# Two-phase kernel on Trainium2: output projection of a batch placed in the next batch's first tail, and end turns without absent groups

## The reference, cut to what matters

```python
q, k, v = (silu(conv4(x @ W)) for W in (Wq, Wk, Wv))   # causal, depthwise
q, k = rope(q), rope(k); q, k = q / norm(q), k / norm(k)
beta, alpha = sigmoid(x @ bw + bb), exp(-exp(A_log) * softplus(x @ gkw + ...))
# per step t:
o_t = q_t S + D * (q_t . k_t) * v_t
S   = alpha_t * (S - beta_t * k_t (k_t S)) + beta_t * k_t v_t
on  = o * rsqrt(mean(o * o) + eps) * onorm_w
s = (g * silu(on)) @ Wo              # g = x @ Wg
```

## Time and profile before

| what | value |
|---|---|
| median of 3 runs | 4598.03 us (4592.21 to 4605.60) |
| the profiled execution | 4639.09 us |
| its span | 4637.3 us, 93208 instructions |
| PE busy | 4129.0 us, 89% |
| PE weight loads | 2724.7 us, 59% |
| DVE / ACT / POOL busy | 65% / 42% / 35% |
| mean granted clock | 0.932 |

### The profile page before, as it was taken

The page is one execution under the profiler, slowest core; times in us unless marked ns, Lnnn a source line. Parts: engine busy times, 40 slices in busy tenths (PEclk is TensorE's granted clock), DMA queues, the critical chain, the costliest instruction groups (busy, mean ns, idle before and its releaser), DMA issues.

```text
span 4637.3 us, 93208 instructions
## 1 busy us (share of the span) xinstructions
PE 4129.0 (89%) x32914; PEld 2724.7 (59%) x32914; DVE 3014.4 (65%) x6409; ACT 1969.6 (42%) x4156; POOL 1644.7 (35%) x1479
## 2 busy tenths in 40 slices
PE   5999998999998989669899899998999989989998
PEld 4444444444444444337667666766666667667666
DVE  3555555555555555377767777867767678678676
ACT  2343334343434343244444534535435445354444
POOL 2111111111111111045545454646554556455454
PEclk9999999999999999888988898988998989989999
DMA  2000000000000000111111111111111111111111
GB/s 97 1 15 1 15 1 15 1 15 1 15 1 15 1 15 1 54 24 39 19 41 26 28 32 23 34 29 30 31 36 19 44 23 30 33 30 23 44 19 34
DMA packets 316505, 110.49 MB, mean 24 GB/s; under 512 B 290096, under 2 KB 303664, under 8 KB 315184
## 3 DMA queue, kind: packets, MB, share of 16 engines
q1 hardware_dynamic: 315968, 103.69, 9.5%
HBM read 77.45 MB, written 26.74 MB: 22 GB/s over the span
## 4 chain that ended last, share of the span: by engine, by line
PE 36%; DVE 11%; issue 4%; ACT 4%; POOL 1%; DMA 1%; SPq 1%; DVEq 0%; POOLq 0%; ACTq 0%
PE d_ps L1778 6%; DVE d_acc L1463 4%; PE d_ps L1854 3%; PE d_ps L1977 3%; PE d_ps L1962 3%; PE d_ps L1997 3%; PE d_ps L1816 2%; PE d_ps L1756 2%; PE d_ps L1833 2%; PE d_ps L1825 1%; PE d_ps L1891 1%; PE d_ps L1905 1%; PE d_ps L1869 1%; DVE d_pw L1566 1%; PE d_ps L1795 1%
## 5 line engine op out<-in xcount | busy, mean ns | idle before, releaser
L228 POOL TENSOR_TENSOR f_qk<-f_m 128x512 f32<-128x512 f32 x128 | 162.8, 1272 | 1538.8 <-DVE f_m L411 1538.7
L1463 DVE SCALAR_TENSOR_TENSOR d_acc<-d_ps,d_cw,d_acc 128x511 f32<-128x511 f32 (+2 forms) x630 | 468.3, 744 | 80.8 <-ACT d_acc L1246 65.0
L1778 PE MATMUL d_ps<-d_xnT,d_wqkv 128*128 128x512 f32 x840 | 488.5, 713 | 0.2 <-DVE d_acc L1463 0.2
L311 ACT ACTIVATE f_pr<-f_sm,f_nb,f_qsc 128x256 f32<-128x256 f32 (+1 forms) x512 | 289.0, 565 | 239.7 <-DVE f_nb L439 237.8
L687 PE MATMUL f_ps<-f_m,f_w 128*128 128x512 f32 (+1 forms) x768 | 338.5, 595 | 22.6 <-DVE f_m L483 22.6
L1246 ACT ACTIVATE d_acc<-d_ps,d_cw 128x512 f32<-128x512 f32 x210 | 162.4, 774 | 406.5 <-PE d_ps L1778 404.6
L1124 POOL TENSOR_TENSOR d_rn<-d_ss,d_mhalf 128x8 f32<-128x8 f32 x137 | 236.5, 1726 | 255.4 <-DVE d_ss L1484 252.3
L433 DVE CUSTOM_DVE_ANT_0 f_sm<-f_ps,f_mask 128x256 f32<-128x256 f32 (+1 forms) x512 | 179.4, 388 | 207.9 <-PE f_ps L603 197.6
L1119 POOL TENSOR_TENSOR d_qk<-d_m 128x512 f32<-128x512 f32 x138 | 174.8, 1267 | 393.4 <-DVE d_m L1474 386.3
L1281 ACT ACTIVATE d_m<-d_qk 128x512 f32<-128x512 f32 x138 | 86.7, 628 | 421.2 <-POOL d_qk L1119 421.2
L687 PEld LDWEIGHTS f_ps<-f_m,f_w 128*128 128x128 f32 (+1 forms) x768 | 134.3, 178 | 223.0 <-issue 187.2
(11 more groups left out here) (210 smaller groups left out, 9675.0 us busy)
## 6 DMA issues: line engine op xcount, KB each, us to landing
d_wqkv<-in_dwqkv SPq DMA_DIRECT2D x36, 768.0 KB, 4.5
blocks_scratch<-d_LT SPq DMA_DIRECT2D x136, 64.0 KB, 2.0
d_T<-inverse_scratch SPq DMA_DIRECT2D x136, 64.0 KB, 2.2
f_xin<-in_x SPq DMA_DIRECT2D x9, 512.0 KB, 4.2
d_xnT<-xnT_scratch SPq DMA_DIRECT2D x9, 512.0 KB, 5.2
d_xnG<-xnT_scratch SPq DMA_DIRECT2D x9, 512.0 KB, 6.6
d_LB<-blocks_scratch SPq DMA_DIRECT2D x68, 64.0 KB, 2.8
inverse_scratch<-d_TB SPq DMA_DIRECT2D x68, 64.0 KB, 4.9
```

The costliest lines, as they stand in the source:

```text
L311: nc.scalar.activation(pr[:, u % 2, j, k0:], sm[:, u % 2, j, k0:], ACT.Exp, bias=nb[:, u % 2, j:j + 1], scale=qsc[:, 0, w, h:h + 1], accum ...
L1463: V.scalar_tensor_tensor(out=a[:, k:], in0=ps[:, CV_BANK[n], 0:T - k], scalar=cw[:, X, s * CT + t, TAPS - 1 - k:TAPS - k], in1=a[:, k:], o ...
L1778: last = mm(ps[:, CV_BANK[n], :], wqkv[:, X, k, t * P:(t + 1) * P], xnT[:, k, :], start=k == 0, stop=k == KC - 1)
```

## The change

It has two parts. The sequence of work is rewritten as a function turn(b, step) on each engine, in which a group that would be outside 0 to 31 is None and its parts are left out. The turns are: step -3 to 0 written out, then a loop over 7 batches with steps 1 to 4 (so the loop's jump comes after the turn s=0 of the next batch), then steps 1 to 3 written out for the last batch. And the output of batch b is placed in the tail of the turn s=0 of batch b + 1; only that of the last batch stays at the end. PE runs the first half of the projection (bank 0) behind convolution item 0, the second half (bank 1) behind item 1, and the transposes, now into banks 0 and 1, behind item 3. To free oT and on, the squares go to a buffer m12 (m1 and m2 side by side), and z is kept in gate. On SP, the store and the next loads of gate and rows stand ahead of inverse_back.

```diff
-    m1 = sb("m1", [P, 2 * GW])
-    m2 = sb("m2", [P, 2 * GW])
+    m12 = sb("m12", [P, 4 * GW])
+    m1, m2 = m12[:, 0:2 * GW], m12[:, 2 * GW:4 * GW]
-    sq = m1
+    sq, osq = m1, m12
-    z = on[:, :, :].rearrange("p (m a) n -> p m (a n)", m=KC)
+    z = gate
+    def group(b, k):
+        if isinstance(b, int) and not 0 <= b * NG + k < B * NG:
+            return None
+        return b * NG + k, k % NG, b + k // NG
+    def late(i, k):
+        return not isinstance(i, int) or i >= k
+    def done(now):
+        return now[2] - 1 if now and now[1] == 0 and late(now[2], 1) else None
     # SP
+        def turn(b, step):
+            now, mid, sub, conv, load = (group(b, step + k) for k in range(5))
+            if sub:
+                inverse_io(sub[0], sub[1] % 2)
+            if conv and load:
+                conv_weights(load[0], load[1])
+            if now and now[1] == 0 and conv:
+                sp.dma_start(flat(xnT), scratch["xnT"][now[2] + 1, :, :, :]).then_inc(xn_in, 16)
...
+            if done(now) is not None:
+                store(done(now))
+                sp.wait_ge(zT_ps, 1 + 2 * now[2])
+                sp.dma_start(flat(gate), scratch["gate"][now[2], :, :, :]).then_inc(gate_in, 16)
+                sp.wait_ge(out_st, 1 + now[2] * 16)
+                sp.dma_start(flat(xio), io["x"][now[2], :, :, :]).then_inc(x_in, 16)
+            if sub:
+                inverse_back(sub[0])
     # ACT, out_heads_T
+            if s == 0 and late(bt, 1):
+                act.wait_ge(wo_ps, 1 + KC * bt)
     # DVE, tail
             if mid: merge16(mid[0])
             conv_items(i, s, range(0, 1))
+            if done(now) is not None: output(done(now), 0)
             conv_items(i, s, range(1, 2))
+            if done(now) is not None: output(done(now), 1)
             merge16_mid, substitute, conv item 2, merge16_end, conv item 3, merge32
+            if done(now) is not None: output_end(done(now))
             substitute_end, merge32_end, ...
     # PE
-                pe.wait_ge(xo_rdy, 1 + 2 * bt)
-        def output(b, i):
-            pe.wait_ge(rf_c, 1 + 2 * (i + 1) + 2)
-            pe.wait_ge(oT_rdy, 1 + b * NG * CT + NG * CT)
-            pe.wait_ge(cv_acc, 1 + val(i + 3, 6, 6))
-            pe.wait_ge(rot_rdy, 1 + 2 * val(i + 3, NT, 2))
+        def output(b, i, m):
+            if m == 0:
+                pe.wait_ge(os_rdy, 1 + val(i, 2 * NT, 2 * NT))
+                pe.wait_ge(oT_rdy, 1 + b * NG * CT + NG * CT)
+            for k in range(H * DH // P):
+                last = mm(ps[:, m, :], wo[:, k, m * P:(m + 1) * P], oT[:, k, :], start=k == 0, stop=k == H * DH // P - 1)
+            last.then_inc(wo_ps, 1)
     # PE, merge32_end
+            if put is not None:
+                pe.wait_ge(xo_rdy, 1 + put * 2 + 2)
     # PE, tail
             conv(*conv_g, 0)
+            if put is not None: output(put, now[0], 0)
             merge16(mid[0], mid[1] % 2, 0)
             conv(*conv_g, 1)
+            if put is not None: output(put, now[0], 1)
             merge16 (second half), g_proj, merge16_end, conv 2, merge16_end, conv 3
+            if put is not None: output_T(put)
             merge32, g_proj, out_heads, merge32_end(mid[0], gated, put), ...
     # every engine
+        for step in range(-3, 1):
+            turn(0, step)
+        with pe.Fori(0, B - 1) as b:
+            for step in range(1, NG + 1):
+                turn(b, step)
+        for step in range(1, NG):
+            turn(B - 1, step)
+        for m in range(KC):
+            output(B - 1, B * NG - 1, m)
+        output_T(B - 1)
```

More of the change, by code:

```diff
@@ new lines, in tail, with turn @@
+            if conv:
+                first_tap(i, s, 4)
+                squares(i, s, bt, 0)
+            if mid:
+                merge64(mid[0])
+            if conv:
+                silu(i, 4)
+                first_tap(i, s, 5)
+            if mid:
+                merge64_end(mid[0])
+            if conv:
+                silu(i, 5)
+                decay_exp(i, s, bt, 0)
+                squares(i, s, bt, 1)
+        def turn(b, step):
+            now, mid, made, conv = (group(b, step + k) for k in range(4))
+            tiles(made, now)
+            tail(conv, mid, now)
@@ L1417, in _ @@
+        act.wait_ge(init1, 1 + 5)
+        for step in range(-3, 1):
+            turn(0, step)
+        with act.Fori(0, B - 1) as b:
+            for step in range(1, NG + 1):
+                turn(b, step)
+        for step in range(1, NG):
+            turn(B - 1, step)
     @block.vector
@@ new lines, in tail @@
+            if conv:
+                i, s, bt = conv
+                conv_items(i, s, range(0, 1))
+            if done(now) is not None:
+                output(done(now), 0)
+            if gated is not None:
+                gates(gated)
+            if conv:
+                conv_items(i, s, range(1, 2))
+            if done(now) is not None:
+                output(done(now), 1)
+            if mid:
+                merge16_mid(mid[0])
+            if sub:
+                substitute(sub[0])
@@ new lines, in tail, with turn @@
+            if conv:
+                intake(i, s, bt, 0)
+                conv_items(i, s, range(4, 5))
+                norms(i, s, bt, 0)
+                intake(i, s, bt, 1)
+                conv_items(i, s, range(5, 6))
+        def turn(b, step):
+            now, mid, made, conv = (group(b, step + k) for k in range(4))
+            tiles(made, now)
+            tail(conv, made, mid, now)
+        dve.wait_ge(init1, 1 + 5)
+        for step in range(-3, 1):
+            turn(0, step)
+        with dve.Fori(0, B - 1) as b:
+            for step in range(1, NG + 1):
+                turn(b, step)
@@ L1726, in _ @@
+        for step in range(1, NG):
+            turn(B - 1, step)
+        for m in range(KC):
+            output(B - 1, m)
+        output_end(B - 1)
     @block.tensor
@@ new lines, in tail, with turn @@
+            if mid:
+                merge64(mid[0], mid[1] % 2)
+            if conv_g:
+                conv(*conv_g, 5)
+                decay_sums(*conv_g, 0)
+            if mid:
+                merge64_end(mid[0])
+        def turn(b, step):
+            now, mid, made, conv_g = (group(b, step + k) for k in range(4))
+            tiles(made, now)
+            tail(conv_g, mid, now)
+        pe.wait_ge(init1, 1 + 5)
+        for step in range(-3, 1):
+            turn(0, step)
+        with pe.Fori(0, B - 1) as b:
+            for step in range(1, NG + 1):
+                turn(b, step)
```

437 lines of the change are left out of this document (189 added, 248 removed).

## The result

The changed kernel takes 4566.85 us (median of 10 runs, 4541.34 to 4594.85) where the kernel before takes 4606.44 beside it (10 runs): a ratio of 0.991 with an interval from 0.988 to 0.994. It is faster, by 40 us where the forecast was 110, and it lies above the range, which ended at 4545.

The account below looks back on a forecast made before the run. The output projection was taken to hold everything up 21.4 us at each batch's end, with PE nearly full in the s=0 tail. Boundary 31, clock 10 and last batch 69 made 110 off 4598: 4488 us, range 4450 to 4545.

Parts of the forecast that it names:

- The sum A to C: Boundary between batches: stall removed, less projection in the s=0 tail and loop's edge, 4.5 a batch, times 7 = 31 us.
- Part A: End of a batch: the stall behind the output projection goes, seven times, mean gain 20.4 us.
- Part B: Tail of s=0: the projection placed there makes the 32-merge 13.5 us late, bounds 13 and 17.5.
- Part C: Loop's jump, now behind an ordinary tail: costs 2.0 to 3.8 us, taken at 2.4, six times.
- the fourth rival: SP's queue: the inverse's write-back waits behind the store, delaying merge16; slower, at say 4649 us; chance 0.02.
- Part D: Turns s=0 after an output: slow spells at 1.2 GHz partly go; gain 10 us, bounds -10 and +45.
- Part E: Last three turns, without absent groups' work: 174.5 us instead of 244, saving 69 (81 at 2.4 GHz, 35 at 1.2).
- the third: Batch boundary gives nothing, costlier edge and full s=0 tail, only the end pays: 4545, or 4529; chance 0.22.
- two blocks of 16: Sign of being right: in s=0 turns, two blocks of 16 projection matmuls behind the first and second convolution.
- L1941 at +32: Sign of being right: the 32-merge (L1891 in before) comes some 32 us into the s=0 tail rather than 19.
- s=3 at 67 to 69: Sign of being right: turns s=3, without the output, take 67 to 69 us.
- s=0 at 85 to 89: Sign of being right: turns s=0, now holding the projection, take 85 to 89 us.

Follow-up runs that it names:

- quiet_s0: Changed kernel with the first batch written out, five jumps behind s=0, SP's large transfers issued only after a turn's first solve: 0.979 of the kernel before.
- the second pair: Changed kernel run once more beside the kernel before, for a second pair of profiles, nothing altered: ratio 0.991.
- before_again: Kernel before run against itself, nothing altered, for a second profile: ratio 1.001.
- the filler: Changed kernel with extra matmuls that nothing reads in PE's gaps of the last three turns: 0.989 of the kernel before.
- loop2: Changed kernel with two batches in one loop body, so two jumps instead of six: 0.983 of the kernel before.

## Why the prediction was wrong

Of the 110 us, 69 were to come from the end and 41 from the boundary and the clock. The end gave 40 to 43, and the boundary and the clock nothing that the times show. Two terms of the sum failed: the loop's edge (C), and the length of the last turns (E). The sum A to C also took the edge seven times where it is crossed six times; its own terms give 34, not 31.

**Part A, the stall goes: right in mechanism, a little too large.** The block of 32 matmuls between turns is gone but in the last; s=3 takes 67.0 to 68.7 in four turns, as forecast, and 71.8 or 71.9 in three. It gives 18.3 a batch in the profile rather than 20.4. Without a jump the stall is 17.0: of my 21.4, the 2.83 of "issue" in the earlier trace rows were the jump, which doesn't go but moves. I had charged it again in part C, so the two terms together are to be compared: 20.4 - 2.4 = 18.0, against 17.0 without a jump. That the other engines use a stall to work ahead (1.7 of tile stage) wasn't in the sum.

**Part B, the projection in the tail of s=0: right.** The 32-merge is 13.1 later than in before, where the tail's first convolution matmul starts at 2466.31; 13.5 were forecast. The wait of merge32_end for the residual additions was put at 0 or 0.6 and is 1.10: DVE's additions follow the copies of L1632 (L1600 in before) directly, and end at 2449.7 while PE is there at 2448.9. The turn is longer by 14.5, inside the bounds of 13 and 17.5. That this tail of PE is full was the right reading, and it was the one to conclude from: taking 17 out of one place and putting 14.5 into another is little to gain.

**Part C, the loop's edge: the term that failed.** I took 2.4, bounds 2.0 and 3.8, from the earlier trace rows. It is 5.4 in the mean at the six jumps. The rows were right for where they stood: in before nothing large had just been issued when PE and DVE came to the jump, since SP issues the store, the gate and the input rows behind the output. quiet_s0 gives 1.9, close to my 2.4. The crowded jump adds to that the 3.0 to 4.5 us by which the packet with PE's code begins late. What I missed is on SP: the four transfers that the new order puts at 2462.94 to 2464.91 were in the diff, and I followed them for what waits on the data, not for what shares the DMA engines. The Trainium skill's page Runtime: NRT & Kernel Launch, section Instruction fetch mechanics, has it that the sequencer fetches code by a DMA queue of its own; by that rule, the traces agree: the packets on q8 above come at the jumps, and not on SP's queue q1. That sentence, laid beside SP's queue, would have given the fourth rival its true victim: it isn't the inverse that comes late, it is the code.

**Part D, the clock: half right.** The slow starts of the turns s=0 did go (their first solve takes 1.08 or 1.20, not 1.92 to 1.97 as in four of seven before). But all six turns s=1 behind a jump now start at 1.2 GHz with a first solve of 1.96 or 1.97, and are 1.7 us longer in the mean (2.7 in the second pair); I had named that and priced it at 5 each. Denser work ended no slow spell in the tails: three turns s=3 still take 71.8 or 71.9. And 26 of gain were counted from a profile whose clock was lower than that of most runs: before_again has 71.0 for the mean turn s=0, not 74.9.

**Part E, the last batch: right in mechanism, mis-sized by the clock.** Forecast 63.5, 50 and 61 together 174.5; measured 67.7, 68.6 and 68.1, together 204.4. With the filler they are 61.6, 51.5 and 54.7: the sums by instruction were sound at the full clock. The step that failed is "19 at full clock, 29 at half; 22 taken": the four tiles of turn 30 take 29.1 and those of turn 31 28.9, and turn 30's merges, put at 28, take 39.5. PE is at 1.2 GHz from 4377 to 4531 nearly without a break, and everything there takes its slow price: the two 16-merges 6.47 for 128 matmuls each, the tiles 8.1 to 8.5. The rest of turn 31 came as forecast, the last projection too (16.29 against 16), since the clock rose at 4531, within it:

```profile
4412.18 1.94 PE L2013 MATMUL d_ps<-d_v,d_Rf 128*128 128x64 f32 x8 [1.31 <-issue]
4414.59 0.69 PE L2023 MATMUL d_ps<-d_us,d_kl 128*64 128x64 f32 x8 [0.47 <-ACT d_us L1325]
4415.21 1.97 PE L2028 MATMUL d_ps<-d_us,d_AT 128*128 128x64 f32 x8
...
4441.33 6.47 PE L1919 MATMUL d_ps<-d_T,d_LT 32*32 32x32 f32 x128
...
4526.41 16.29 PE L2047 MATMUL d_ps<-d_oT,d_wo 128*128 128x512 f32 x32 [0.78 <-ACT d_oT L1340]
```

My bound for all at 1.2 GHz was a saving of 35; 39.5 and 43.4 were measured. Taking the convolutions out of a turn takes out the work that had kept PE busy, and the rest takes a third longer (turn 30: 68.6 against 51.5). I had both ends and took a value near the wrong one.

**The rivals.** Nearest is the third (the boundary gives nothing, only the end pays), at 4529 to 4545; it had this kernel's course, but still the full 69 of the end. With 40 for the end it gives 4598 - 40 = 4558 from the three runs shown, and 4566 from the median of ten: the result. Its chance of 0.22 was too small against 0.55: with a tail that I had just called full and an edge bounded by the mildest case in the trace, the gain of 4.5 a batch was less than the spread of its own terms. The range ended at 4545 because every rival that it took in kept the end at its full 69: the boundary and the clock were allowed to go wrong, the end never.

Of the signs named: two blocks of 16, L1941 at +32, s=3 at 67 to 69 and s=0 at 85 to 89 came nearly so (six of the seven s=0 took 88.6 to 93.3, one of them over the 93 that was named as a sign of being wrong); the last turns and the mean clock under 0.9 there (0.77, 0.52, 0.63) told the other way. PE shows no gap ahead of merge16 in the tail of s=1, so SP's queue did not delay the inverse.

## What to carry to other kernels

Ahead of moving work off a batch's end, look for a tail in which the bounding engine waits: here the full one (s=0) gave 2.5 us of 17, its neighbour with a wait of 6.24 took the same 14 us of matmuls for 3.4. A loop's jump costs what the fetch of code costs at that moment, so issue the large transfers behind it, or put it where other work covers it. And price what is left after a cut at the clock that the thinned stretch will be granted, not at that of the full one.

## What was unexpected of the hardware

- A jump of all engines costs 1.9 us beyond an ordinary hand-over when the DMA engines are free and 5.4 when 2.25 MB have been issued within the last 3 us before it. The difference is the time by which the fetch of PE's code starts late behind these transfers; the fetch itself takes about 1 us in both.
- Work that PE does for nothing can shorten a stretch: with 133 more matmuls in the last two turns they took 106 us instead of 137, and the granted clock rose from 0.52 and 0.63 to 0.93 and 0.98. Over three pairs of runs the times fall by 0.002 to 0.006 of before's, where the traces fall by 0.007 or 0.008.
- Written-out turns are shorter than looped ones also without a jump: 82.7 against mostly 84.4 to 84.7 for s=0 (one looped turn of loop2 took 82.1), and 1.31 instead of 1.50 to 1.67 idle at each start. The waits on constants instead of computed values may be the cause; no run took that alone.
